# Down projection of a quantised feed-forward: half-tile quantisation moved to GpSimd, and a new order of casts

## The chip, the cores and the metric

The kernel runs on one core of a Trainium2 chip. The metric is the device time of one launch in microseconds (us). The kernel before was timed in three runs: median 204.54 us, from 204.34 to 204.71.

## The reference, cut to what matters

The input x is (32, 128, 256) float32. Two residual layers follow one another: a gated, two-directional RWKV mix of a context with weights `w` and `u`, and a quantised feed-forward. Only the second one, and of it only its last projection, is touched here:

```
x  = x + tanh(g_xattn) * birwkv(layernorm(x), ctx, ctx, w, u)
xq = fake_quant(layernorm(x))                  # one scale for the whole tensor
h  = silu(xq @ Wg.T) * (xq @ Wu.T)             # 4096 tokens x 704
s  = sigmoid(clip_down) * max|h| / 127         # one scale for the whole tensor
hq = clip(round(h / s), -128, 127) * s
x  = x + tanh(g_ffn) * hq @ fake_quant(Wd).T   # 704 -> 256
```

`max|h|` is taken over everything, so nothing of the last product can begin before all of h is there. The weights are quantised as h is, with a scale for each row.

## The kernel before, in words

The program is written engine by engine, with semaphores set and awaited by hand; there is no scheduler, and each engine does its instructions in the order in which they are written. The stages are: statistics and exponentials of the context, the mixing by matrix products (until about 102 us), the second layernorm and its transposes (to about 124 us), gate and up products with silu and the peaks of h (to about 172 us), and then the down stage, which is all that changes.

**The down stage** works on 4 blocks of 1024 tokens (`BLOCKS`), each with 4 outputs of 256 tokens (`OUTS`), 16 outputs in all (`SUMS`). The 704 hidden values stand as 5 full tiles of 128 (`KI`) and a last tile of 64, the *half tile*. Of that one, the two halves of a block's tokens lie above one another, so it is one instruction of 128x512 for the whole block; the 5 full tiles of an output are one instruction of 128x1280, of an output pair 128x2560.

For each piece there are two steps:

- Quantise (L709 on ScalarE, L970 on VectorE): float32 `hidden` times the inverse scale, written as int16, which rounds. The list `QUANTS` has the pieces in the order in which ScalarE does them, as (block, first output, end, first tile, end). `BY_DVE` names the pieces that VectorE quantises itself: the first two, and the half tile of block 1.
- Cast (L986, `cast_h`, VectorE): clip to -128..127 and write bf16. The list `CASTS` is its order. For the half tiles and for outputs 0 and 1 of block 0, source and destination are the same place in `hq` (`z_t` in the trace). All other outputs go through `pair_int`, two buffers of an output pair in `h8_space`, so the cast reads `h_space` in rows of 256 and writes `z_t`.

TensorE then makes an output (`down`, L1183) from 12 products of 128x256. VectorE scales it out of PSUM (`evict`, L992). GpSimd adds it to `x_all` (L502) for the outputs 0 to 14, and SyncE sends each of these out (L358). VectorE itself adds output 15 (L998), whose transfer ScalarE's queue issues (L713).

**Order on VectorE** (L1000 to L1016): before `evict(n)` it casts all that `needed(n + 2)` asks for (for n = 0 and 1, `needed(n + 1)`). `needed` (L195) is a position in `CASTS`: a block's half tile must be cast before its output 0. So the order runs evict 1, quantise and cast half tile 1, cast output 3, cast output 4, evict 2; later evict 5, cast half tile 2, cast output 8, evict 6; and evict 9, cast half tile 3, cast output 12, evict 10. TensorE waits at output n for the same `needed(n)` casts (L1176).

**Order on ScalarE** (L710): `QUANTS`. Before the first piece of an output pair from pair 3 on it waits until the pair two before has been cast. Outputs 4 and 5 are single pieces, outputs 6 and 7 one pair. From block 2 on, the half tile comes first, then two pairs.

**Order on GpSimd** (L499): the adds 0 to 14 and nothing else, each behind `ffn_done`, which the eviction of the same output sets.

Semaphores that the change touches: `h_int` (pieces quantised by ScalarE), `h_int_own` (by VectorE), `hq_done` (casts done), `down_done` (outputs made by TensorE), `inv_done` (the inverse scale is there).

Of the kernel before, what the change touches and what calls it, by code (L numbers as in the profile page):

```python
# [22 lines left out]
ALU = mybir.AluOpType  # L23
# [5 lines left out]
I16 = mybir.dt.int16  # L29
# [6 lines left out]
def wait(engine, semaphore, value):  # L36

    if isinstance(value, int) and value <= 0:
        return
    engine.wait_ge(semaphore, value)  # L40

def gated_rwkv_ffn(nc, x, ctx_kv, g_xattn, g_ffn, w, u, clip_x, clip_down, w_gate, w_up, w_down, out):
# [8 lines left out]
    KI = I // P  # L51
    IR = I - KI * P
    KA = KI + 1
    BT = 1024
    BLOCKS = TOK // BT
# [16 lines left out]
    with ExitStack() as stack:  # L72
# [3 lines left out]
        def sem(name):  # L76
            return stack.enter_context(nc.semaphore(name))
# [95 lines left out]
        def z_bank(g):  # L173
            return (2, 6, 0)[g % 3]

        OUTS = BT // 256
        OUT = KI * 256

        CASTS = [(0, 0, 0, 2), (0, 0, 2, 4), (0, 0, 4, KI), (0, 0, KI, KA), (0, 1, 0, KI), (0, 2, 0, KI), (1, 0, KI, KA), (0, 3, 0, KI)] \
            + [c for b in range(1, BLOCKS) for c in ([(b, 0, KI, KA)] if b > 1 else []) + [(b, i, 0, KI) for i in range(OUTS)]]  # L180

        QUANTS = [(0, 0, 1, 4, KI), (0, 0, OUTS, KI, KA), (0, 1, 2, 0, KI), (0, 2, 3, 0, KI), (0, 3, 4, 0, KI),
                  (1, 0, 1, 0, KI), (1, 1, 2, 0, KI), (1, 2, 4, 0, KI)] \
            + [q for b in range(2, BLOCKS) for q in [(b, 0, OUTS, KI, KA), (b, 0, 2, 0, KI), (b, 2, 4, 0, KI)]]
        BY_DVE = [0, 1, CASTS.index((1, 0, KI, KA))]

        def kept(b, i, k, end):

            if k == KI:
                return hq[b % 2][:, OUTS * OUT:HB]  # L190
            return hq[b % 2][:, i * OUT + k * 256:i * OUT + end * 256]

        def inner(b, i, last, k, end):

            if k == KI:  # L195
                return hidden[:, b * HB + KI * BT:(b + 1) * HB]
            return hidden[:, b * HB:b * HB + KI * BT].rearrange("p (k n) -> p k n", n=BT)[:, k:end, i * 256:last * 256]

        def needed(n):

            return 1 + max(m for m, (b, i, k, _) in enumerate(CASTS) if b == n // OUTS and i == n % OUTS or b < n // OUTS
                           or b == n // OUTS and k == KI)
# [12 lines left out]
        def group(tile, g):  # L215
# [5 lines left out]
        S = {n: small[:, i:i + 1] for i, n in enumerate(names)}  # L221
# [21 lines left out]
        s = {n: sem(n) for n in (  # L243

            "gate_in", "up_in", "down_in", "g_x_in", "g_f_in", "clx_in", "cld_in", "w_in", "u_in",
            "ones_set", "ident_set", "flip_set", "lags_set", "lag_done", "lag_stored", "lag_abs_set", "lag_abs_done", "w_all_in", "u_all_in", "u_all_done", "own_done", "made_exp", "made",
            "tanh_done", "clips_done", "prep",

            "w_rec", "w_quant", "w_cast", "w_turned", "w_stored",

            "ctx_back", "ek_done", "pk_done", "ab_done", "den_done", "ln_done", "rden_done", "ln_half", "rden_half", "mix_done", "x1_done", "x1_own",
# [6 lines left out]
            "scale_x", "inv_x_done", "x_int_own", "x_int_act", "x_int_pool", "xq_done", "gate_done", "up_done", "silu_done", "up_kept", "h_even", "h_odd",  # L258
            "hpeak_done", "h_top_done", "h_topT", "row_ps",

            "inv_done", "h_int", "h_int_own", "hq_done", "pad_set", "diag_done", "row_kept", "down_done", "ffn_done", "sum_done", "dve_sum_done", "out_done")}

        x_in = [sem(f"x_in{g}") for g in range(GROUPS)]
        ring_in = [sem(f"ring_in{i}") for i in range(SLOTS)]
# [97 lines left out]
        def _(pool):  # L362
# [114 lines left out]
            def quantise_x(n):  # L477

                pool.wait_ge(s["x_int_own"], 3)
                pool.wait_ge(s["x_int_act"], 2)  # L480
                nc.gpsimd.tensor_scalar(x_int(n), x_normed(n), S["inv_x"], 1.0, ALU.mult, ALU.mult).then_inc(s["x_int_pool"], 1)
# [10 lines left out]
            for b in range(BLOCKS):  # L492
                for i in range(EVEN):
                    multiply(b, i)
                if b == 0:
                    for n in X_BY_POOL[2:]:
                        quantise_x(n)

            for n in pool_sums:  # L499
                pool.wait_ge(s["ffn_done"], n + 1)  # L500
                xs = x_all[:, n * 2 * C:(n + 1) * 2 * C]
                nc.gpsimd.tensor_tensor(xs, xs, ffn[n // 4 % 2][:, n % 4, :], ALU.add).then_inc(s["sum_done"], 1)  # L502
# [3 lines left out]
        def _(act):  # L506
# [190 lines left out]
            act.wait_ge(s["inv_done"], 1)  # L697
            for b, i, last, k, end in QUANTS:
                pair, first = (b * OUTS + i) // 2, i % 2 * 256
                if k == KI:  # L700
                    wait(act, s["down_done"], OUTS * (b - 1))
                    dst = kept(b, i, k, end).bitcast(I16)
                elif pair == 0:
                    dst = kept(b, i, k, end).bitcast(I16).rearrange("p (k n) -> p k n", n=256)
                else:
                    if pair >= 3 and first == 0:
                        act.wait_ge(s["hq_done"], needed(2 * (pair - 2) + 1))
                    dst = pair_int[pair % 2][:, :, first:first + (last - i) * 256]
                nc.scalar.activation(dst, inner(b, i, last, k, end), ACT.Copy, scale=S["inv_h"]).then_inc(s["h_int"], 1)  # L709
# [7 lines left out]
        def _(dve):  # L717
# [250 lines left out]
            def quantise_h(b, i, k, end):  # L968
                dst = kept(b, i, k, end).bitcast(I16)
                nc.vector.tensor_scalar(dst if k == KI else dst.rearrange("p (k n) -> p k n", n=256), inner(b, i, i + 1, k, end),  # L970
                                        S["inv_h"], None, ALU.mult).then_inc(s["h_int_own"], 1)

            def cast_h(n):

                b, i, k, end = CASTS[n]
                dst = kept(b, i, k, end)
                src = dst.bitcast(I16)
                if n in BY_DVE:
                    dve.wait_ge(s["h_int_own"], BY_DVE.index(n) + 1)
                else:  # L980
                    done = [m for m, (at_, first, last, k0, k1) in enumerate(QUANTS)
                            if at_ == b and (k0, k1) == (k, end) and first <= i < last]
                    dve.wait_ge(s["h_int"], done[0] + 1)
                if k < KI and b * OUTS + i >= 2:
                    src = pair_int[(b * OUTS + i) // 2 % 2][:, :, i % 2 * 256:(i % 2 + 1) * 256]
                nc.vector.tensor_scalar(dst, src, QMAX, -QMAX - 1.0, ALU.min, ALU.max).then_inc(s["hq_done"], 1)  # L986

            def evict(n):
                dve.wait_ge(s["down_done"], n + 1)
                wait(dve, s["sum_done"], len([i for i in pool_sums if i <= n - 8]))  # L990
                dst = ps[:, n % 8, :] if n in dve_sums else ffn[n // 4 % 2][:, n % 4, :]
                nc.vector.scalar_tensor_tensor(dst, ps[:, n % 8, :], S["out_scale"], flat_row, ALU.mult, ALU.mult) \  # L992
                    .then_inc(s["ffn_done"], 1)

            def add_rest(n):
                dve.wait_ge(s["ffn_done"], n + 1)
                xs = x_all[:, n * 2 * C:(n + 1) * 2 * C]
                nc.vector.tensor_tensor(xs, xs, ps[:, n % 8, :], ALU.add).then_inc(s["dve_sum_done"], 1)  # L998

            cast = 0  # L1000
            for n in BY_DVE[0:2]:
                quantise_h(*CASTS[n])
                cast_h(n)
                cast += 1
# [2 lines left out]
            dve.wait_ge(s["row_kept"], 1)  # L1007
            for n in range(SUMS):
                while cast < needed(min(n + (1 if n < 2 else 2), SUMS - 1)):
                    if cast == BY_DVE[2]:  # L1010
                        quantise_h(*CASTS[cast])
                    cast_h(cast)
                    cast += 1
                evict(n)
                if n in dve_sums:
                    add_rest(n)  # L1016
# [195 lines left out]
```

## Time and profile before

| | |
|---|---|
| median of three runs | 204.54 us |
| the profiled execution | 204.7 us |
| its span | 203.0 us (1.7 us lie around it) |
| mean granted TensorE clock | 0.946 |
| TensorE busy, matmul | 172.6 us (85%) |
| VectorE busy | 158.7 us (78%) |
| ScalarE busy | 150.9 us (74%) |
| GpSimd busy | 123.3 us (61%) |

Times in the trace count from the start of the span. The busy times are sums over stages with different limits; the down stage is the stretch from about 172 us to the end. In the trace DVE is VectorE, ACT is ScalarE, POOL is GpSimd, PE is TensorE and SP is SyncE. A row of the timeline may join several instructions of a kind that follow one another closely (x2, x3); its time is then that from the first one's start to the last one's end.

### The profile page before, as it was taken

How to read it: one execution, taken by the hardware profiler on the slowest of the kernel's cores; microseconds unless marked ns; L12 is line 12 of the kernel's file. 1: busy time of each engine (PE TensorE's matmuls, PEld its weight loads, DVE VectorE, ACT ScalarE, POOL GpSimd, SP SyncE). 2: the span in 40 equal slices, each digit the busy share in tenths (PEclk: the TensorE clock that was granted, in tenths of full speed). 3: DMA queues.
4: the chain of work that ended last, by engine and by line, in shares of the span. 5: the costliest groups of instructions: out<-in, count | busy, mean ns of one | idle time of the engine just before them, and what ended most of it. 6: DMA issues, size and time to landing. Idle time of an engine off the chain costs nothing.

```text
span 203.0 us, 3345 instructions
## 1 busy us (share of the span) xinstructions
PE 172.6 (85%) x1146; PEld 126.3 (62%) x1146; DVE 158.7 (78%) x355; ACT 150.9 (74%) x219; POOL 123.3 (61%) x149
## 2 busy tenths in 40 slices
PE   4589995997999999999137998999999996869990
PEld 4447642997989999999136664444343442558770
DVE  0657769174955878998969957599999998999992
ACT  3447969857599379558879998999888980999900
POOL 3365303467869936354788850889876762258892
PEclk9958999999999999999955599999999999999998
DMA  2999999999999999990000000000000000034555
GB/s 73 353 338 353 348 341 292 294 297 289 294 290 323 238 289 293 290 243 0 2 0 0 0 3 2 0 0 0 3 0 0 0 0 0 3 103 164 198 171 195
DMA packets 46448, 30.88 MB, mean 152 GB/s; under 512 B 2272, under 2 KB 46176, under 8 KB 46432
## 3 DMA queue, kind: packets, MB, share of 16 engines
q1 hardware_dynamic: 46016, 30.16, 53.0%
q10 hardware_dynamic: 416, 0.52, 0.7%
q8 instruction: 9, 0.15, 0.3%
q14 instruction: 7, 0.06, 0.1%
HBM read 26.22 MB, written 4.46 MB: 151 GB/s over the span
## 4 chain that ended last, share of the span: by engine, by line
PE 40%; DVE 29%; DMA 10%; ACT 7%; issue 6%; POOL 4%; SPq 1%; POOLq 1%; DVEq 0%
PE ps L1044 21%; DMA hidden<-lag_w 6%; PE ps L1147 6%; DVE h_peaks L937 6%; DVE z_t L986 6%; PE ps L1028 5%; DVE hidden L926 4%; DMA hidden<-in_ctx 4%; PE ps L1075 3%; PE ps L1068 2%; DVE bn L755 2%; DVE z_t L992 2%; DVE hidden L729 2%; DVE silu_out L992 2%; POOL rs L398 2%
## 5 line engine op out<-in xcount | busy, mean ns | idle before, releaser
L1044 PE MATMUL ps<-hidden 128*128 128x128 f32 (+1 forms) x512 | 58.4, 275 | 4.2 <-DVE hidden L729 2.5
L1044 PEld LDWEIGHTS ps<-hidden 128*128 128x128 f32 x512 | 57.7, 192 | 5.4 <-issue 3.3
L428 POOL TENSOR_TENSOR x_all<-x_all,silu_out 128x512 f32<-128x512 f32 x15 | 23.0, 1533 | 17.2 <-DVE silu_out L798 17.2
L937 DVE TENSOR_REDUCE h_peaks<-hidden 128x1 f32<-128x1024 f32 (+1 forms) x24 | 26.1, 1124 | 0.2
L1183 PE MATMUL ps<-wdT,z_t 128*128 128x256 bf16 x192 | 22.4, 272 | 2.8 <-DVE z_t L986 2.5
L786 DVE SCALAR_TENSOR_TENSOR h_space<-z_t,ps 128x256 f32<-128x256 f32 x32 | 18.9, 595 | 7.1 <-PE ps L1044 6.8
L1183 PEld LDWEIGHTS ps<-wdT,z_t 128*128 128x128 bf16 x192 | 17.8, 97 | 7.6 <-DVE z_t L986 3.2
L689 ACT ACTIVATE silu_out<-ps,mix_scale 128x1024 f32<-128x1024 f32 (+1 forms) x18 | 18.3, 1019 | 2.1 <-PE ps L1147 2.0
L1068 PE MATMUL ps<-ident,hidden 128*128 128x128 f32 x64 | 12.1, 352 | 8.9 <-POOL hidden L467 8.2
L1028 PE MATMUL ps<-hidden,flip 128*128 128x512 f32 x32 | 16.7, 662 | 3.3 <-DMA hidden<-in_ctx 3.3
L798 DVE SCALAR_TENSOR_TENSOR silu_out<-ps,small,silu_out 128x256 f32<-128x256 f32 x32 | 15.2, 478 | 5.2 <-ACT silu_out L545 4.6
L534 ACT ACTIVATE z_t<-x_all,mr,nr 128x256 f32<-128x256 f32 x32 | 16.4, 588 | 3.7 <-POOL mr L390 3.7
L747 DVE BATCH_NORM_STATS2 bn<-x_all 128x6 f32<-128x256 f32 x32 | 11.2, 413 | 8.7 <-DMA x_all<-in_x 8.4
L1068 PEld LDWEIGHTS ps<-ident,hidden 128*128 128x128 f32 x64 | 10.2, 185 | 11.5 <-ACT hidden L564 10.0
L709 ACT ACTIVATE h_space<-hidden,small 128x2560 int16<-128x2560 f32 (+1 forms) x9 | 17.1, 1943 | 0.3 <-DVE z_t L986 0.3
L542 ACT ACTIVATE up_out<-h_space 128x512 f32<-128x512 f32 x15 | 9.4, 626 | 10.5 <-DVE h_space L786 10.5
L487 POOL TENSOR_TENSOR hidden<-h_space 128x1024 f32<-128x1024 f32 x6 | 14.7, 2449 | 3.9 <-ACT h_space L693 3.9
L502 POOL TENSOR_TENSOR x_all<-x_all,z_t 128x512 f32<-128x512 f32 x8 | 10.4, 1296 | 10.3 <-DVE z_t L992 9.9
L487 POOL TENSOR_TENSOR hidden<-silu_out,up_out 128x1024 f32<-128x1024 f32 x6 | 14.2, 2363 | 3.8 <-ACT up_out L693 3.8
L926 DVE SCALAR_TENSOR_TENSOR hidden<-ps,mix_scale,silu_out 128x1024 f32<-128x1024 f32 (+1 forms) x12 | 13.2, 1101 | 2.9 <-ACT silu_out L689 2.8
L385 POOL TENSOR_TENSOR ve<-mv,consts 128x4 f32<-128x4 f32 x8 | 1.6, 199 | 21.9 <-DVE mv L751 21.9
L1075 PEld LDWEIGHTS ps<-ident,flip 128*128 128x128 f32 x64 | 10.9, 256 | 5.3 <-POOL ident_b L374 2.8
(117 smaller groups left out, 346.1 us busy)
## 6 DMA issues: line engine op xcount, KB each, us to landing
hidden<-lag_w SPq DMA_DIRECT2D x29, 512.0 KB, 7.4
x_all<-in_x SPq DMA_DIRECT2D x8, 512.0 KB, 8.8
hidden<-in_ctx SPq DMA_DIRECT2D x8, 512.0 KB, 9.3
out<-x_all SPq DMA_DIRECT2D x15, 256.0 KB, 2.1
xq<-in_L_ffn_w_down SPq DMA_DIRECT2D x1, 704.0 KB, 6.1
xq<-in_L_ffn_w_gate SPq DMA_DIRECT2D x1, 640.0 KB, 6.8
h_space<-in_L_ffn_w_up SPq DMA_DIRECT2D x1, 640.0 KB, 5.9
out<-x_all ACTq DMA_DIRECT2D x1, 256.0 KB, 2.7
```

What stands on the lines that cost most here:

```text
L428: nc.gpsimd.tensor_tensor(xs, xs, mixed[:, m % 2, :, :].rearrange("p c b -> p b c"), ALU.add).then_inc(s["x1_done"], 1)
L487: nc.gpsimd.tensor_tensor(hidden[:, b * HB + k * BT:b * HB + (k + 1) * BT], silu_even[n % 2], up_even[n % 2], ALU.mult).then_inc(s["h_even ...
L689: nc.scalar.activation(silu_out[:, 1, 0:cols] if k % 2 else silu_even[even % 2], banks[0], ACT.Silu, scale=mix_scale[:, 0, k:k + 1]).then_ ...
L709: nc.scalar.activation(dst, inner(b, i, last, k, end), ACT.Copy, scale=S["inv_h"]).then_inc(s["h_int"], 1)
L786: nc.vector.scalar_tensor_tensor(den[:, m % 2, i * HALF:(i + 1) * HALF].rearrange("p (c b) -> p c b", b=SEQS), ez[:, :, j * CK:(j + 1) * C ...
L926: nc.vector.scalar_tensor_tensor(hidden[:, b * HB + k * BT:b * HB + k * BT + cols], ps[:, 6:8, :].rearrange("p a n -> p (a n)")[:, 0:cols] ...
L937: nc.vector.tensor_reduce(h_peaks[:, KA * b + k:KA * b + k + 1], hidden[:, b * HB + k * BT:b * HB + k * BT + cols], AX.X, ALU.max, apply_a ...
L1028: last = nc.tensor.matmul(turned(g)[:, half], flip[:, :], ring[g % SLOTS][:, half], start=True, stop=True)
L1044: last = nc.tensor.matmul(ps[:, j % BANKS, c * 2 * SEQS:end * 2 * SEQS], lag_tile(j)[:, c, :], ekp[:, (j * CK + c) * 2 * SEQS:(j * CK + en ...
L1068: last = nc.tensor.transpose(ps[:, z_bank(g) + h, i * T:(i + 1) * T], z_all[:, n * C + h * P:n * C + (h + 1) * P], ident[:, :])
L1075: nc.tensor.matmul(ps[:, TURN, 0:P], flip[:, :], ident[:, :], start=True, stop=True)
L1183: last = nc.tensor.matmul(ps[:, n % 8, j * C:(j + 1) * C], hq[b % 2][:, at_:at_ + P], wdT[:, tile, :], start=(k == 0 and j == 0), stop=(k ...
```

## The change

The half tiles of blocks 1, 2 and 3 are quantised by GpSimd, by a `tensor_scalar` of 128x512 in a new function `quantise_half`. It does the one of block 1 before its first add, as soon as the inverse scale is there and three casts are done; that of block 2 between the adds 3 and 4; that of block 3 between the adds 8 and 9. VectorE's casts of these tiles wait on the new semaphore `h_int_pool`. VectorE no longer quantises half tile 1, and ScalarE no longer those of blocks 2 and 3. In `CASTS`, output 3 now stands ahead of half tile 1. In `QUANTS`, the outputs 6 and 7 are two single pieces instead of a pair.

```diff
--- before.py
+++ after.py
@@ -176,13 +176,14 @@
         OUTS = BT // 256
         OUT = KI * 256
 
-        CASTS = [(0, 0, 0, 2), (0, 0, 2, 4), (0, 0, 4, KI), (0, 0, KI, KA), (0, 1, 0, KI), (0, 2, 0, KI), (1, 0, KI, KA), (0, 3, 0, KI)] \
-            + [c for b in range(1, BLOCKS) for c in ([(b, 0, KI, KA)] if b > 1 else []) + [(b, i, 0, KI) for i in range(OUTS)]]
-
-        QUANTS = [(0, 0, 1, 4, KI), (0, 0, OUTS, KI, KA), (0, 1, 2, 0, KI), (0, 2, 3, 0, KI), (0, 3, 4, 0, KI),
-                  (1, 0, 1, 0, KI), (1, 1, 2, 0, KI), (1, 2, 4, 0, KI)] \
-            + [q for b in range(2, BLOCKS) for q in [(b, 0, OUTS, KI, KA), (b, 0, 2, 0, KI), (b, 2, 4, 0, KI)]]
-        BY_DVE = [0, 1, CASTS.index((1, 0, KI, KA))]
+        CASTS = [(0, 0, 0, 2), (0, 0, 2, 4), (0, 0, 4, KI), (0, 0, KI, KA)] + [(0, i, 0, KI) for i in range(1, OUTS)] \
+            + [c for b in range(1, BLOCKS) for c in [(b, 0, KI, KA)] + [(b, i, 0, KI) for i in range(OUTS)]]
+
+
+        QUANTS = [(0, 0, 1, 4, KI), (0, 0, OUTS, KI, KA)] + [(0, i, i + 1, 0, KI) for i in range(1, OUTS)] \
+            + [(1, i, i + 1, 0, KI) for i in range(OUTS)] \
+            + [(b, i, i + 2, 0, KI) for b in range(2, BLOCKS) for i in range(0, OUTS, 2)]
+        BY_DVE = [0, 1]
 
         def kept(b, i, k, end):
 
@@ -258,7 +259,7 @@
             "scale_x", "inv_x_done", "x_int_own", "x_int_act", "x_int_pool", "xq_done", "gate_done", "up_done", "silu_done", "up_kept", "h_even", "h_odd",
             "hpeak_done", "h_top_done", "h_topT", "row_ps",
 
-            "inv_done", "h_int", "h_int_own", "hq_done", "pad_set", "diag_done", "row_kept", "down_done", "ffn_done", "sum_done", "dve_sum_done", "out_done")}
+            "inv_done", "h_int", "h_int_own", "h_int_pool", "hq_done", "pad_set", "diag_done", "row_kept", "down_done", "ffn_done", "sum_done", "dve_sum_done", "out_done")}
 
         x_in = [sem(f"x_in{g}") for g in range(GROUPS)]
         ring_in = [sem(f"ring_in{i}") for i in range(SLOTS)]
@@ -496,7 +497,18 @@
                     for n in X_BY_POOL[2:]:
                         quantise_x(n)
 
+            def quantise_half(b):
+
+                wait(pool, s["down_done"], OUTS * (b - 1))
+                nc.gpsimd.tensor_scalar(kept(b, 0, KI, KA).bitcast(I16), inner(b, 0, OUTS, KI, KA), S["inv_h"], 1.0,
+                                        ALU.mult, ALU.mult).then_inc(s["h_int_pool"], 1)
+
+            pool.wait_ge(s["inv_done"], 1)
+            pool.wait_ge(s["hq_done"], 3)
+            quantise_half(1)
             for n in pool_sums:
+                if n in (OUTS, 2 * OUTS + 1):
+                    quantise_half(2 + n // (2 * OUTS))
                 pool.wait_ge(s["ffn_done"], n + 1)
                 xs = x_all[:, n * 2 * C:(n + 1) * 2 * C]
                 nc.gpsimd.tensor_tensor(xs, xs, ffn[n // 4 % 2][:, n % 4, :], ALU.add).then_inc(s["sum_done"], 1)
@@ -698,7 +710,6 @@
             for b, i, last, k, end in QUANTS:
                 pair, first = (b * OUTS + i) // 2, i % 2 * 256
                 if k == KI:
-                    wait(act, s["down_done"], OUTS * (b - 1))
                     dst = kept(b, i, k, end).bitcast(I16)
                 elif pair == 0:
                     dst = kept(b, i, k, end).bitcast(I16).rearrange("p (k n) -> p k n", n=256)
@@ -977,6 +988,8 @@
                 src = dst.bitcast(I16)
                 if n in BY_DVE:
                     dve.wait_ge(s["h_int_own"], BY_DVE.index(n) + 1)
+                elif k == KI and b > 0:
+                    dve.wait_ge(s["h_int_pool"], b)
                 else:
                     done = [m for m, (at_, first, last, k0, k1) in enumerate(QUANTS)
                             if at_ == b and (k0, k1) == (k, end) and first <= i < last]
@@ -998,7 +1011,7 @@
                 nc.vector.tensor_tensor(xs, xs, ps[:, n % 8, :], ALU.add).then_inc(s["dve_sum_done"], 1)
 
             cast = 0
-            for n in BY_DVE[0:2]:
+            for n in BY_DVE:
                 quantise_h(*CASTS[n])
                 cast_h(n)
                 cast += 1
@@ -1007,8 +1020,6 @@
             dve.wait_ge(s["row_kept"], 1)
             for n in range(SUMS):
                 while cast < needed(min(n + (1 if n < 2 else 2), SUMS - 1)):
-                    if cast == BY_DVE[2]:
-                        quantise_h(*CASTS[cast])
                     cast_h(cast)
                     cast += 1
                 evict(n)
```

## Rows read from the trace of the kernel before

**Rows 1.** Busy time in one stretch: PE, PEld, DVE, ACT, POOL, clock, DMA share, GB/s.
```profile
179.84:197.80 17.96, 17.80 (x156) 14.60 (x156) 17.62 (x28) 13.02 (x7) 14.94 (x12) 1.00 0.48 163
```

**Rows 2.** Waits from 172 us to the end: us in total, times, longest.
```profile
PE ps L1183 <- DVE z_t L986: 2.5, 3, 1.7
...
DVE ps L992 <- PE ps L1183: 0.3, 1, 0.3
```

**Rows 3.** Timeline of DVE, first outputs: start, duration, instruction, idle before.
```profile
173.86 0.43 DVE L986 TENSOR_SCALAR z_t<-z_t 128x256 bf16<-128x256 int16 x2
174.56 0.49 DVE L986 TENSOR_SCALAR z_t<-z_t 128x1280 bf16<-128x1280 int16 x1 [0.28 <-ACT z_t L709]
...
176.64 0.75 DVE L992 SCALAR_TENSOR_TENSOR z_t<-ps,small,down_row 128x512 f32<-128x512 f32 x1
177.30 0.48 DVE L970 TENSOR_SCALAR z_t<-hidden,small 128x512 int16<-128x512 f32 x1
177.82 1.24 DVE L986 TENSOR_SCALAR z_t<-z_t 128x512 bf16<-128x512 int16 x1
178.98 1.53 DVE L986 TENSOR_SCALAR z_t<-h_space 128x1280 bf16<-128x1280 int16 x2
180.43 0.73 DVE L992 SCALAR_TENSOR_TENSOR z_t<-ps,small,down_row 128x512 f32<-128x512 f32 x1
```

**Rows 4.** Timeline of DVE around half tile 2.
```profile
183.20 0.73 DVE L992 SCALAR_TENSOR_TENSOR silu_out<-ps,small,down_row 128x512 f32<-128x512 f32 x1
...
184.59 0.73 DVE L992 SCALAR_TENSOR_TENSOR silu_out<-ps,small,down_row 128x512 f32<-128x512 f32 x1
185.25 0.27 DVE L986 TENSOR_SCALAR z_t<-z_t 128x512 bf16<-128x512 int16 x1
185.44 0.80 DVE L986 TENSOR_SCALAR z_t<-h_space 128x1280 bf16<-128x1280 int16 x1
186.17 0.73 DVE L992 SCALAR_TENSOR_TENSOR silu_out<-ps,small,down_row 128x512 f32<-128x512 f32 x1
```

**Rows 5.** Timeline of POOL in the down stage.
```profile
175.80 1.28 POOL L502 TENSOR_TENSOR x_all<-x_all,z_t 128x512 f32<-128x512 f32 x1 [6.86 <-DVE z_t L992]
177.47 1.44 POOL L502 TENSOR_TENSOR x_all<-x_all,z_t 128x512 f32<-128x512 f32 x1 [0.39 <-DVE z_t L992]
...
195.49 3.87 POOL L502 TENSOR_TENSOR x_all<-x_all,silu_out 128x512 f32<-128x512 f32 x3
```

**Rows 6.** POOL's multiplications L487 (ns min/median/max), and the timeline at its longest.
```profile
L487 POOL TENSOR_TENSOR hidden<-h_space x6: 2357/2368/2869, 132.9 to 166.6; 128x1024 f32<-128x1024 f32 x6
...
132.90 0.68 DVE L907 TENSOR_SCALAR z_t<-z_t 128x2048 bf16<-128x2048 int16 x1
...
132.94 2.87 POOL L487 TENSOR_TENSOR hidden<-h_space 128x1024 f32<-128x1024 f32 x1 [0.28 <-ACT h_space L693]
```

**Rows 7.** POOL's three forms of tensor_scalar: ns min/median/max, first and last start.
```profile
L450 POOL TENSOR_SCALAR xq<-xq x1: 405/405/405, 41.0 to 41.0; 128x256 f32<-128x256 f32 x1
...
L467 POOL TENSOR_SCALAR hidden<-x_all,rs,mr x8: 548/554/557, 104.0 to 119.5; 128x256 f32<-128x256 f32 x8
...
L481 POOL TENSOR_SCALAR z_t<-z_t,small x4: 1107/1120/1615, 127.6 to 139.8; 128x1024 int16<-128x1024 f32 x4
```

**Rows 8.** Timeline of PE, last half of output 1.
```profile
175.78 0.82 PE L1183 MATMUL ps<-wdT,z_t 128*128 128x256 bf16 x6
```

**Rows 9.** Timeline: POOL's own pace, and VectorE released by POOL.
```profile
138.74 2.21 POOL L481 TENSOR_SCALAR z_t<-z_t,small 128x1024 int16<-128x1024 f32 x2
...
108.98 0.55 POOL L467 TENSOR_SCALAR hidden<-x_all,rs,mr 128x256 f32<-128x256 f32 x1
...
109.64 1.22 DVE L813 TENSOR_REDUCE peaks<-hidden 128x1 f32<-128x1024 f32 x1 [0.23 <-POOL hidden L467]
```

**Rows 10.** Timeline of ACT in the down stage.
```profile
174.44 5.11 ACT L709 ACTIVATE h_space<-hidden,small 128x1280 int16<-128x1280 f32 x4
...
182.15 0.71 ACT L709 ACTIVATE z_t<-hidden,small 128x512 int16<-128x512 f32 x1
```

## Prediction

> **What bounds the kernel now.** I read the busy shares first, then the down stage: its busy times, its waits, and the timelines of VectorE, GpSimd and ScalarE there. From 179.84 us to the last product VectorE is busy 17.62 of 17.96 us, TensorE 17.80, GpSimd 14.94, ScalarE 13.02 [rows 1]. Two engines look full, and the waits decide between them: VectorE waits for TensorE only 0.3 us, once, at the last output, while TensorE waits for VectorE's casts 2.5 us, 1.7 of them in one piece [rows 2]. So VectorE's order of casts and evictions sets the pace: an eviction every 1.39 us (183.20 to 184.59), and 1.58 us where a half tile is cast between (184.59 to 186.17) [rows 4]. Whatever moves one eviction moves all that follow, down to the last transfer, since VectorE has no idle time in which to make it up. GpSimd's adds take 1.28 us and start 0.83 us after the start of their eviction (176.64 to 177.47) [rows 3, 5], so they end 0.11 us before the next is due: close, but behind VectorE. The last three, back to back, end at 195.49 + 3.87 = 199.36 us [rows 5].
>
> The row to look at is the cast of half tile 1: 1.24 us at 177.82, where the same form takes 0.27 at 185.25 [rows 3, 4]. GpSimd's add ran from 177.47 to 178.91, and the cast ended 0.15 us behind it. The other way round, a multiplication of GpSimd that began 0.04 us after a contiguous cast of VectorE took 2.87 us against a median of 2.37 [rows 6]. So a contiguous cast of VectorE and an instruction of GpSimd exclude one another. The casts of output 3 and later read `h_space` in rows of 256, and take 0.80 us with an add beside them: they don't meet it.
>
> **The change, part by part.** I count by the starts of evictions.
>
> *A GpSimd half tile.* No row has this form (128x512, float32 to int16). The nearest: 128x256 at 0.405 and 0.55, and the same operation at 128x1024 at 1.107 [rows 7]. I take 0.65, near the straight line between 0.405 and 1.107 (0.64); these two are the ends. Below nothing it can't go, since VectorE waits for it.
>
> *Start, half tile 1.* GpSimd waits for the third cast, in the pair that ends at 174.29 [rows 3]; so about 174.1, plus 0.09 to wake: its tile runs from 174.2 to about 174.85. The cast of output 1, contiguous too, is issued at 174.56 and would be held until then; it ends 0.15 us later as half tile 1 does, plus 0.20, by which its form is longer (0.49 against 0.29): 175.20 against 175.05. Eviction 0 slips by as much and is covered by the wait for ScalarE's output 2. Eviction 1 is not: TensorE ends output 1 at 176.60 [rows 8], now 176.75. Cost 0.15 us; bounds 0 and 0.61 by the ends above.
>
> *The turn to block 1.* Now: eviction 1 at 176.64, quantise 0.48, held cast until 179.06, casts of outputs 3 and 4, eviction 2 at 180.43 [rows 3]. After: eviction 1 at 176.79, then output 3's cast, which runs beside add 1 at no cost; add 1 from 177.62 to 178.90 (1.28, as VectorE's quantise no longer stretches it to 1.44); the half tile's cast is issued in it, is held, ends at 179.05; then only one cast, starting 0.08 before that end, 0.73 long: eviction 2 at 179.70. Gain 0.73 us. TensorE's wait of 1.7 us for output 3 shrinks, which alone is worth nothing, since VectorE is late behind it.
>
> *Half tile 2.* With eviction 5 as zero: add 3 from -1.95 to -0.67, GpSimd's tile to -0.02, add 4 to 1.26. VectorE issues its cast at 0.66, in the middle of add 4, while before the cast fell between two adds, and took 0.27 us [rows 4]. Now held, it ends at 1.41, and eviction 6 comes 0.65 later, at 2.06 instead of 1.58. Cost 0.48 us.
>
> *Half tile 3.* It stands one add later. With eviction 9 as zero: add 8 from -0.56 to 0.72, the tile to 1.37, but VectorE wants to cast it at 0.66. It must wait for the semaphore, and behind it on VectorE stand the cast of output 12 and eviction 10, on which TensorE and add 10 wait. At 1.37 add 9 has long been released (eviction 9 ended at 0.74). GpSimd starts a ready instruction with no gap (2.21 us for two of 1.107), VectorE woke 0.11 us after GpSimd's end (108.98 + 0.55 = 109.53, start 109.64) [rows 9]. So add 9 is there first and holds the cast until 1.37 + 1.28 = 2.65; it ends at 2.80, eviction 10 at 3.45 instead of 1.58. Cost 1.87 us.
>
> The trace has no case in which both want to start at once; here a rule bears on it. The Trainium skill, "SBUF — State Buffer", section "Who interferes with whom", says that issue order alone decides which of the two gets the shared pair of ports, for its whole instruction. The trace agrees in the two collisions [rows 3, 5, 6]. By the rule the cost is the 1.87 us above; if VectorE's waiting cast went first whatever the order, it would be 0.82, the rival below.
>
> *ScalarE.* It loses two half tiles (0.71 us each) and does outputs 6 and 7 singly, at some 1.25 each [rows 10]: output 6 is ready at about 180.8, needed at 181.7; output 7 at 182.1, needed at 183.1. It costs nothing, and gains nothing, since VectorE waited for it only at 174.56. Were this cover gone, its lateness would show in full on VectorE's casts; there is near 1 us of it.
>
> *Added waits on GpSimd.* `down_done` is met in both places, as the add before implies it. Transfers move with their adds. At the end GpSimd has caught up, since VectorE was held longer than it: nothing.
>
> **Sum.** -0.73 + 0.48 + 1.87 = +1.62 us on the profiled execution: span 203.0 to 204.6, time 204.7 to 206.3. The profile lies 0.16 above the median of 204.54, so 206.2. With 0.405 us for the tile: -0.88 + 0.23 + 1.63 = +0.98, 205.5. With 1.107: -0.27 + 0.94 + 2.33 = +3.0, 207.5. The second needs a half tile as dear as a double one.
>
> **Rivals.**
>
> *A. VectorE's cast of half tile 3 gets in before add 9.* Then it starts at 1.48, and eviction 10 follows 0.92 after the cast's start as in [rows 4]: 2.40, cost 0.82, sum +0.57: 205.1. For it: the margin is 0.1 us of semaphore and start-up times that no row shows for this pair. Against: [rows 9].
>
> *B. GpSimd's queue keeps the port.* At half tile 2, add 5 is ready when add 4 ends; in the collisions of the trace nothing was ready behind. If add 5 also passes the held cast, another 1.28 us: sum +2.9, 207.4. Against: VectorE has been asking for 0.6 us by then.
>
> *C. Faster: nothing is held.* If the 1.24 us of the cast were something else, bound to that place, then: no 0.15, output 3's cast at 177.30, the half tile's at 178.03, output 4 ready from ScalarE at 178.3 [rows 10], eviction 2 at 179.05, a gain of 1.38; nothing at half tile 2; 0.82 at half tile 3. Sum -0.56: 204.0. It decides if a contiguous cast under an add takes 0.3 us. Against: two independent pairs of rows that agree to 0.1 us.
>
> *D. No difference.* A tile near 0.4 us together with A: -0.88 + 0.23 + 0.58 = -0.07, 204.5.
>
> **How the numbers follow.** Forecast (add 9 first, VectorE next at half tile 2) 0.62; A 0.18; B 0.07; C 0.07; D and other mixtures 0.06. Range 204.9 to 207.2: it takes in the forecast, A, and a tile up to about 1.0 us, and leaves out B, C and D. Of changes of this kernel 0.2% (0.4 us) can be told from none. Slower: forecast, B and most of A, 0.84. Within: D and the rest of A, 0.09. Faster: C, 0.07.
>
> **What would show it.** In the trace after: GpSimd's `tensor_scalar` of 128x512 at about 0.65 us, three times; eviction 2 about 0.7 us earlier; the cast of half tile 2 recorded at about 0.75 us; idle time on VectorE before the cast of half tile 3, and that cast itself over 1 us, with eviction 10 some 3.4 us after eviction 9; a gap of about 1.9 us on TensorE before output 12. I am wrong if the cast of half tile 3 takes 0.3 us (A), if that of half tile 2 takes 2 us (B), or if half tile 1's takes 0.3 us beside an add (C). And if evictions from 10 on come closer than 1.39 us, VectorE was not the bound.

## The result, and the profile after

The changed kernel takes 206.09 us (median of five runs, 205.77 to 206.96) against 204.54 us before (204.09 to 205.36). The ratio, taken over all runs, is 1.0092, with a 95% interval of 1.0061 to 1.0122: slower by 1.9 us, 1.2 to 2.5. (The two medians differ by 1.55 us.) The forecast was 206.2, the range 204.9 to 207.2. The profiled execution took 206.96 us, its span is 204.8 us; it is the slowest of the five, and 0.23 us of its distance to the kernel before lie ahead of the down stage.

Part of the loss stands in no timeline. The time of a launch is longer than its span, and this rest grew: it is 2.07 to 2.19 us in the five runs of the changed kernel (mean 2.12), and 1.68 to 1.86 us in the runs of the kernel before that were timed beside the experiments (mean 1.74). So the change costs 0.38 us outside the span besides what it costs in the down stage. The ratios and these means leave out three slow executions (355.81 us of e4, 301.24 and 207.03 us of the kernel before).

Single executions of these kernels differ by some tenths of a per cent. The steps are therefore read inside the down stage. Zero is the start of VectorE's first quantise of h; a number behind a half tile is its block, and output n, its eviction n and its add n belong together. These are the zero and the turn to block 3 in the timeline of VectorE, for the kernel before:

```profile
172.22 0.49 DVE L970 TENSOR_SCALAR z_t<-hidden,small 128x512 int16<-128x512 f32 x1
...
190.33 0.73 DVE L992 SCALAR_TENSOR_TENSOR z_t<-ps,small,down_row 128x512 f32<-128x512 f32 x1
190.99 0.27 DVE L986 TENSOR_SCALAR z_t<-z_t 128x512 bf16<-128x512 int16 x1
...
191.91 0.73 DVE L992 SCALAR_TENSOR_TENSOR z_t<-ps,small,down_row 128x512 f32<-128x512 f32 x1
```

The same timeline of the changed kernel. L981 is the quantise, L999 the cast, L1005 the eviction; these rows answer to [rows 3, 4]:

```profile
172.45 0.49 DVE L981 TENSOR_SCALAR z_t<-hidden,small 128x512 int16<-128x512 f32 x1
...
174.80 0.73 DVE L999 TENSOR_SCALAR z_t<-z_t 128x1280 bf16<-128x1280 int16 x1 [0.28 <-ACT z_t L720]
...
177.11 0.75 DVE L1005 SCALAR_TENSOR_TENSOR z_t<-ps,small,down_row 128x512 f32<-128x512 f32 x1 [0.20 <-PE ps L1194]
177.78 0.81 DVE L999 TENSOR_SCALAR z_t<-h_space 128x1280 bf16<-128x1280 int16 x1
178.51 0.86 DVE L999 TENSOR_SCALAR z_t<-z_t 128x512 bf16<-128x512 int16 x1
179.29 0.81 DVE L999 TENSOR_SCALAR z_t<-h_space 128x1280 bf16<-128x1280 int16 x1
180.02 0.74 DVE L1005 SCALAR_TENSOR_TENSOR z_t<-ps,small,down_row 128x512 f32<-128x512 f32 x1
...
184.17 0.74 DVE L1005 SCALAR_TENSOR_TENSOR silu_out<-ps,small,down_row 128x512 f32<-128x512 f32 x1
184.83 0.72 DVE L999 TENSOR_SCALAR z_t<-z_t 128x512 bf16<-128x512 int16 x1
...
186.20 0.73 DVE L1005 SCALAR_TENSOR_TENSOR silu_out<-ps,small,down_row 128x512 f32<-128x512 f32 x1
...
190.35 0.73 DVE L1005 SCALAR_TENSOR_TENSOR z_t<-ps,small,down_row 128x512 f32<-128x512 f32 x1
191.76 1.35 DVE L999 TENSOR_SCALAR z_t<-z_t 128x512 bf16<-128x512 int16 x1 [0.67 <-POOL z_t L503]
193.03 0.81 DVE L999 TENSOR_SCALAR z_t<-h_space 128x1280 bf16<-128x1280 int16 x1
193.76 0.73 DVE L1005 SCALAR_TENSOR_TENSOR z_t<-ps,small,down_row 128x512 f32<-128x512 f32 x1
```

Eviction 2 comes at 7.57 us from zero instead of 8.21 (0.64 gained). Evictions 5 and 6 are 2.03 us apart instead of 1.58 (0.45 lost), evictions 9 and 10 3.41 instead of 1.58 (1.83 lost). Eviction 10 is at 21.31 instead of 19.69: 1.62 us later, and this stays to the end of VectorE's last instruction (28.68 us from zero instead of 27.06).

GpSimd's timeline shows what each long cast ran into. L503 is the new quantise, L514 the add; these rows answer to [rows 5]:

```profile
174.50 0.69 POOL L503 TENSOR_SCALAR z_t<-hidden,small 128x512 int16<-128x512 f32 x1 [5.32 <-DVE z_t L999]
...
177.94 1.27 POOL L514 TENSOR_TENSOR x_all<-x_all,z_t 128x512 f32<-128x512 f32 x1 [0.39 <-DVE z_t L1005]
...
183.47 0.69 POOL L503 TENSOR_SCALAR z_t<-hidden,small 128x512 int16<-128x512 f32 x1
...
184.13 1.27 POOL L514 TENSOR_TENSOR x_all<-x_all,silu_out 128x512 f32<-128x512 f32 x1
...
185.36 1.31 POOL L514 TENSOR_TENSOR x_all<-x_all,silu_out 128x512 f32<-128x512 f32 x1
...
191.03 0.69 POOL L503 TENSOR_SCALAR z_t<-hidden,small 128x512 int16<-128x512 f32 x1
191.69 1.27 POOL L514 TENSOR_TENSOR x_all<-x_all,z_t 128x512 f32<-128x512 f32 x1
```

Every cast of a `z_t` piece that begins beside one of these instructions ends 0.15 to 0.34 us behind it: the cast of output 1 behind the tile (175.53 and 175.19), those of half tiles 1, 2 and 3 behind adds 1 (179.37 and 179.21), 4 (185.55 and 185.40) and 9 (193.11 and 192.96). The 14 casts out of `h_space` take 0.802 to 0.807 us, with adds beside them (least, median and most in ns):

```profile
L999 DVE TENSOR_SCALAR z_t<-h_space x14: 802/804/807, 176.1 to 197.2; 128x1280 bf16<-128x1280 int16 x14
L999 DVE TENSOR_SCALAR z_t<-z_t x8: 227/509/1354, 173.0 to 191.8; 128x512 bf16<-128x512 int16 x6, 128x256 bf16<-128x256 int16 x1, 128x1280 bf16<-128x1280 int16 x1
```

TensorE waits for output 12's cast, its one long gap of the stage (idle time in brackets):

```profile
193.99 0.71 PE L1194 MATMUL ps<-wdT,z_t 128*128 128x256 bf16 x5 [1.94 <-DVE z_t L999]
```

### The profile page after: what moved, and what is told of

It reads as the page before. It is cut to its first block, busy times and chain, and to the rows that moved or that the text cites. A ratio compares the mean times of both kernels' runs of the same rounds, so it can differ in the third digit from the quotient of the medians.

```text
span 204.8 us, 3347 instructions
## 1 busy us (share of the span) xinstructions
PE 171.3 (84%) x1146; PEld 124.7 (61%) x1146; DVE 159.7 (78%) x354; ACT 149.8 (73%) x218; POOL 125.1 (61%) x152
## 4 chain that ended last, share of the span: by engine, by line
PE 37%; DVE 26%; DMA 10%; ACT 8%; SPq 6%; issue 5%; POOL 5%; POOLq 1%; DVEq 0%
PE ps L1055 18%; PE ps L1039 8%; PE ps L1158 6%; DMA hidden<-lag_w 6%; DVE h_peaks L948 6%; DVE z_t L999 5%; DVE hidden L937 4%; DMA hidden<-in_ctx 4%; ACT hidden L576 3%; PE ps L1086 3%; SPq L306 2%; DVE bn L766 2%; POOL x_all L514 2%; ACT z_t L583 2%; DVE z_t L1005 2%
## 5 line engine op out<-in xcount | busy, mean ns | idle before, releaser
L1194 PE MATMUL ps<-wdT,z_t 128*128 128x256 bf16 x192 | 22.9, 273 | 3.9 <-DVE z_t L999 3.8
L720 ACT ACTIVATE h_space<-hidden,small 128x1280 int16<-128x1280 f32 (+1 forms) x10 | 17.1, 1777 | 1.1 <-DVE z_t L999 1.1
L766 DVE BATCH_NORM_STATS2 bn<-x_all 128x6 f32<-128x128 f32 x64 | 13.6, 279 | 0.1
L1086 PEld LDWEIGHTS ps<-ident,flip 128*128 128x128 f32 x64 | 10.3, 242 | 5.3 <-POOL ident_b L375 2.8
```

The source lines that it names most:

```text
L766: return nc.vector.bn_stats(bn2[:, n, h, :], x_all[:, n * C + h * P:n * C + (h + 1) * P])
L1194: last = nc.tensor.matmul(ps[:, n % 8, j * C:(j + 1) * C], hq[b % 2][:, at_:at_ + P], wdT[:, tile, :], start=(k == 0 and j == 0), stop=(k ...
```

## The experiments

All times "from zero" are as above, each from one trace. The ratios are to the kernel before, timed again beside the experiments (medians 204.44 us beside e1, e2, e3 and e6, and 204.30 us beside e4, e5 and e7), with their 95% intervals. "The port" in the expectations is the way to the on-chip memory that VectorE and GpSimd are taken to share.

**Half tile 3 one add earlier (e1).** The changed kernel, with this edit:

```diff
-                if n in (OUTS, 2 * OUTS + 1):
+                if n in (OUTS, 2 * OUTS):
                     quantise_half(2 + n // (2 * OUTS))
```

> The changed kernel with half tile 3 quantised by GpSimd before add 8 instead of before add 9. Theory (an add of GpSimd and a contiguous cast of VectorE exclude one another, whoever starts first): with eviction 9 as zero the tile ends at 0.0, add 8 runs from 0.0 to 1.28, the cast is issued at 0.66, is held, ends at 1.42; eviction 10 at 2.05 instead of 3.41 us, as at half tile 2. The whole comes 1.36 us below the changed kernel, about 204.7 us. Rival (what costs is only that the tile comes too late, 0.67 us of waiting and what follows from it; the port plays no part): the tile is there 0.66 us early, so nothing is left of the cost, eviction 10 at 1.58, the whole 1.83 us below, 204.3 us. Second rival (GpSimd's load as such sets the pace): no difference to the changed kernel.

Measured: 204.99 us, ratio 1.0039 (1.0011 to 1.0067). The timeline of VectorE and GpSimd at the turn to block 3:

```profile
189.84 1.27 POOL L514 TENSOR_TENSOR x_all<-x_all,z_t 128x512 f32<-128x512 f32 x1
189.89 0.73 DVE L1005 SCALAR_TENSOR_TENSOR z_t<-ps,small,down_row 128x512 f32<-128x512 f32 x1
...
190.55 0.71 DVE L999 TENSOR_SCALAR z_t<-z_t 128x512 bf16<-128x512 int16 x1
191.07 1.32 POOL L514 TENSOR_TENSOR x_all<-x_all,z_t 128x512 f32<-128x512 f32 x1
...
191.91 0.74 DVE L1005 SCALAR_TENSOR_TENSOR z_t<-ps,small,down_row 128x512 f32<-128x512 f32 x1
```

The evictions 9 and 10 are 2.02 us apart: 2.05 by the port, 1.58 if only lateness cost, 3.41 if GpSimd's load did. The run's time agrees once the rest outside the span is counted: eviction 10 is 0.22 us behind the kernel before, the rest is 2.09 us instead of 1.74, together 0.57 us; measured are 0.2 to 1.4 us by the ratio. The tile had long been there (its quantise began at 189.18 and took 0.70), and VectorE shows no wait; the cast is long because add 8 runs. The rows also settle a point that the prediction left to a rival. Add 9 was ready when add 8 ended at 191.11, since eviction 9 had ended at 190.62. The cast ended at 191.26 all the same, 0.15 us behind add 8 and not one add later, and add 9 is recorded with 1.32 instead of 1.27 us. The waiting cast had its turn first.

**Add 9 made to wait for the cast (e2).** The changed kernel, with one wait more:

```diff
                     quantise_half(2 + n // (2 * OUTS))
+                if n == 2 * OUTS + 1:
+                    pool.wait_ge(s["hq_done"], CASTS.index((3, 0, KI, KA)) + 1)
                 pool.wait_ge(s["ffn_done"], n + 1)
```

> The changed kernel, with one more wait: GpSimd starts add 9 only when VectorE has cast half tile 3. Theory (add 9 holds the port for 1.28 us when the cast wants it): the cast starts 0.04 us behind the tile, at 1.41 from eviction 9, takes 0.27 to 0.29 us instead of 1.35, and eviction 10 comes at 2.33 instead of 3.41 us; about 1.1 us below the changed kernel, 205.0 us. Rival (the cast takes 1.35 us because GpSimd has written its source just before, or for another reason of its own): the cast stays at 1.3 us, eviction 10 at 3.4 or later, no gain. In both, add 9 starts late, at about 1.8, and nothing waits for it.

Measured: 205.54 us, ratio 1.0045 (1.0023 to 1.0068). The timeline at the same turn:

```profile
190.47 0.73 DVE L1007 SCALAR_TENSOR_TENSOR z_t<-ps,small,down_row 128x512 f32<-128x512 f32 x1
...
191.15 0.70 POOL L503 TENSOR_SCALAR z_t<-hidden,small 128x512 int16<-128x512 f32 x1
191.88 0.29 DVE L1001 TENSOR_SCALAR z_t<-z_t 128x512 bf16<-128x512 int16 x1 [0.68 <-POOL z_t L503]
...
192.26 1.28 POOL L516 TENSOR_TENSOR x_all<-x_all,z_t 128x512 f32<-128x512 f32 x1 [0.41 <-DVE z_t L1001]
...
192.82 0.74 DVE L1007 SCALAR_TENSOR_TENSOR z_t<-ps,small,down_row 128x512 f32<-128x512 f32 x1
```

The cast of the same tile, written by the same engine just before, takes 0.29 us instead of 1.35 once nothing of GpSimd runs beside it, and eviction 10 comes 2.35 us after eviction 9 (2.33 expected). So 1.83 us of cost divide into 1.06 for the held cast and 0.77 for the tile that comes late. A wait put in made the stage faster than that of the changed kernel. The median lies 0.5 us above the 205.0 that was expected, which was reckoned from the changed kernel's median of five runs. Eviction 10, at 20.25, is 1.06 below the changed kernel as expected. Reckoned from the kernel before, the time fits: 0.56 us in the down stage and 0.27 outside the span (2.01 us against 1.74) make a ratio of 1.0041, measured 1.0045. So the 0.5 us lie in the spread of the changed kernel's few runs, as far as the record shows.

**Half tiles 2 and 3 back on ScalarE (e3).** Only the first part of the change is left. ScalarE does every output from block 1 on singly.

```diff
-            + [(b, i, i + 2, 0, KI) for b in range(2, BLOCKS) for i in range(0, OUTS, 2)]
+            + [q for b in range(2, BLOCKS) for q in [(b, 0, OUTS, KI, KA)] + [(b, i, i + 1, 0, KI) for i in range(OUTS)]]
...
-                if n in (OUTS, 2 * OUTS + 1):
-                    quantise_half(2 + n // (2 * OUTS))
...
                 if k == KI:
+                    wait(act, s["down_done"], OUTS * (b - 1))
...
-                elif k == KI and b > 0:
+                elif k == KI and b == 1:
```

> The changed kernel with half tiles 2 and 3 back on ScalarE, and all outputs from block 1 on quantised singly there; only half tile 1 stays on GpSimd, and output 3 is still cast ahead of it. Theory: the first part of the change gains 0.64 us by itself and the other two tiles cost 0.45 and 1.83 us, so evictions 5 to 6 and 9 to 10 are 1.58 us apart again, and the whole is 2.3 us below the changed kernel and 0.64 below the kernel before: about 203.9 us. Rival (ScalarE had no room, so the tiles had to leave it): ScalarE needs 4 x 1.25 + 0.61 = 5.6 us for a block and VectorE 5.75, so it can't fall behind by this count; if it does, VectorE shows waits for ScalarE before the casts of block 2, and the gain shrinks by their sum.

Measured: 203.88 us, ratio 0.9979 (0.9958 to 1.0000). The timeline of VectorE at the turn to block 2:

```profile
184.11 0.74 DVE L1004 SCALAR_TENSOR_TENSOR silu_out<-ps,small,down_row 128x512 f32<-128x512 f32 x1
184.77 0.28 DVE L998 TENSOR_SCALAR z_t<-z_t 128x512 bf16<-128x512 int16 x1
...
185.70 0.74 DVE L1004 SCALAR_TENSOR_TENSOR silu_out<-ps,small,down_row 128x512 f32<-128x512 f32 x1
```

Evictions 5 to 6 and 9 to 10 are 1.59 us apart, eviction 2 is at 7.56, eviction 10 at 19.04, 0.65 ahead of the kernel before. VectorE never waits for ScalarE in blocks 1 to 3. The whole loss of the change sits in the two later tiles, and so does the longer rest outside the span: it is back at 1.76 us. The run's time by itself hardly tells e3 from no change, as the interval ends at 1.0000; the trace does.

**The order of casts alone (e6).** The kernel before, VectorE still quantising half tile 1:

```diff
-        CASTS = [..., (0, 2, 0, KI), (1, 0, KI, KA), (0, 3, 0, KI)] \
+        CASTS = [..., (0, 2, 0, KI), (0, 3, 0, KI), (1, 0, KI, KA)] \
```

> The kernel before with only the order of casts changed: output 3 ahead of half tile 1, which VectorE still quantises itself. Theory: output 3's cast (0.73 us) runs under add 1; then VectorE's own quantise, which is contiguous too, is issued in the last 0.7 us of the add and held until it ends, 178.75 on the clock of the kernel before; it ends at 179.04, its cast at 179.33, and eviction 2 comes at about 179.98 instead of 180.43: 0.45 us gained of the 0.64 that the changed kernel gained there, about 204.1 us. Rival (the gain is that of the quantise that VectorE no longer does, 0.52 us, and the order is worth nothing because TensorE has room): eviction 2 at 180.4, no difference.

Measured: 204.07 us, ratio 0.9984 (0.9958 to 1.0009): the run's time can't tell it from no change, the trace can. Its timeline of VectorE, first output 3's cast, then the quantise (L970) and the cast of half tile 1, and GpSimd's add 1:

```profile
177.22 0.81 DVE L986 TENSOR_SCALAR z_t<-h_space 128x1280 bf16<-128x1280 int16 x1
177.38 1.27 POOL L502 TENSOR_TENSOR x_all<-x_all,z_t 128x512 f32<-128x512 f32 x1 [0.40 <-DVE z_t L992]
177.95 0.99 DVE L970 TENSOR_SCALAR z_t<-hidden,small 128x512 int16<-128x512 f32 x1
178.97 0.29 DVE L986 TENSOR_SCALAR z_t<-z_t 128x512 bf16<-128x512 int16 x1
```

Eviction 2 is at 7.78 from zero (8.21 before): 0.43 of the 0.64 us come from the order, because output 3's cast fills time in which a contiguous piece would be held anyway. The quantise itself is now held: it takes 0.99 us against 0.48 and ends at 178.94, 0.29 us behind add 1. So VectorE's contiguous quantise is held as the cast is, in the one case traced.

**GpSimd's half tile 1 behind the cast of output 1 (e4).** As e3, with this edit:

```diff
-            pool.wait_ge(s["hq_done"], 3)
+            pool.wait_ge(s["hq_done"], 5)
             quantise_half(1)
```

> As e3, but GpSimd starts half tile 1 only behind the fifth cast (output 1), not the third. Zero is the first quantise of VectorE. Theory: output 1's cast is no longer held (0.49 us instead of 0.73), half tile 1 runs in GpSimd's idle time from 2.9 to 3.6, just ahead of add 0, and eviction 1 comes at 4.42 as in the kernel before instead of 4.66; eviction 2, still behind the held cast, at 7.33 instead of 7.56: 0.23 us below e3. Rival (eviction 1 is late for another reason, as TensorE's pace): eviction 1 stays at 4.66.

Measured: 203.40 us, ratio 0.9949 (0.9931 to 0.9968). The timeline of VectorE and GpSimd at the cast of output 1 and the tile:

```profile
174.85 0.49 DVE L998 TENSOR_SCALAR z_t<-z_t 128x1280 bf16<-128x1280 int16 x1 [0.28 <-ACT z_t L719]
...
175.52 0.69 POOL L503 TENSOR_SCALAR z_t<-hidden,small 128x512 int16<-128x512 f32 x1 [6.31 <-DVE z_t L998]
```

The cast of output 1 takes 0.49 us again, eviction 1 is at 4.42 and eviction 2 at 7.33. So the tile's early start did cost 0.24 us at eviction 1 (4.66 in the changed kernel).

**And half tile 1 cast ahead of output 3 (e5).** As e4, with the order of casts of the kernel before:

```diff
-        CASTS = [...] + [(0, i, 0, KI) for i in range(1, OUTS)] \
-            + [c for b in range(1, BLOCKS) for c in [(b, 0, KI, KA)] + [(b, i, 0, KI) for i in range(OUTS)]]
+        CASTS = [...] + [(0, 1, 0, KI), (0, 2, 0, KI), (1, 0, KI, KA), (0, 3, 0, KI)] \
+            + [c for b in range(1, BLOCKS) for c in ([(b, 0, KI, KA)] if b > 1 else []) + [(b, i, 0, KI) for i in range(OUTS)]]
```

> As e4, but with the order of casts of the kernel before: half tile 1 ahead of output 3. Theory: the cast of the half tile is issued right behind eviction 1, in the gap before add 1, and takes 0.28 us instead of being held; eviction 2 comes at 4.42 + 0.66 + 0.19 + 0.73 + 0.73 = 6.73, or at 6.83 with the wait for output 4 from ScalarE (ready at 6.07), against 8.21 in the kernel before and 7.33 in e4: 1.4 us below the kernel before, about 203.1 us. Rival (output 3 must come first, as the change has it, or TensorE runs late): eviction 2 or 3 waits for TensorE, and the gain over e4 is lost. Second rival (the GpSimd tile grips the port all the same): the cast stays above 0.8 us.

Measured: 202.82 us, ratio 0.9935 (0.9914 to 0.9956), the lowest median of all. Its timeline, of VectorE and of GpSimd's add 1:

```profile
173.19 0.49 DVE L980 TENSOR_SCALAR z_t<-hidden,small 128x512 int16<-128x512 f32 x1
...
177.64 0.75 DVE L1004 SCALAR_TENSOR_TENSOR z_t<-ps,small,down_row 128x512 f32<-128x512 f32 x1
178.31 0.28 DVE L998 TENSOR_SCALAR z_t<-z_t 128x512 bf16<-128x512 int16 x1
178.47 1.27 POOL L512 TENSOR_TENSOR x_all<-x_all,z_t 128x512 f32<-128x512 f32 x1 [0.34 <-DVE z_t L1004]
...
180.03 0.74 DVE L1004 SCALAR_TENSOR_TENSOR z_t<-ps,small,down_row 128x512 f32<-128x512 f32 x1
```

The cast starts behind eviction 1 and 0.16 us ahead of add 1, and takes 0.28 us. It ends 0.12 us behind the add's start, and the add takes its usual 1.27 us. Eviction 2 is at 6.84 (6.83 expected), 1.37 us ahead of the kernel before, and no eviction waits for TensorE but the last. The order "output 3 first" of the change is the worse one as soon as GpSimd, and not VectorE, quantises the tile early. By eviction 2 this beats e4 by 0.49 us and by the medians by 0.6; the intervals of the two ratios overlap, so their order rests on the traces.

**Single pieces on ScalarE alone (e7).** The kernel before with this edit:

```diff
-                  (1, 0, 1, 0, KI), (1, 1, 2, 0, KI), (1, 2, 4, 0, KI)] \
-            + [q for b in range(2, BLOCKS) for q in [(b, 0, OUTS, KI, KA), (b, 0, 2, 0, KI), (b, 2, 4, 0, KI)]]
+                  (1, 0, 1, 0, KI), (1, 1, 2, 0, KI), (1, 2, 3, 0, KI), (1, 3, 4, 0, KI)] \
+            + [q for b in range(2, BLOCKS) for q in [(b, 0, OUTS, KI, KA)] + [(b, i, i + 1, 0, KI) for i in range(OUTS)]]
```

> The kernel before with only ScalarE's list changed: from output 6 on all outputs are quantised singly instead of in pairs. Theory: ScalarE is ahead of VectorE either way, so every eviction stays where it is, eviction 2 at 8.21 and eviction 10 at 19.69 from the first quantise, to 0.05 us. Rival (single pieces cost ScalarE 0.17 us per pair, and its lead is thin, so VectorE begins to wait for it in block 2): eviction 10 some tenths later.

Measured: 204.10 us, ratio 0.9994 (0.9970 to 1.0018). Eviction 2 at 8.22, eviction 10 at 19.70: nothing, as expected. So the gains of e3, e4 and e5 don't come from ScalarE's list.

| from zero, us | eviction 1 | eviction 2 | 5 to 6 | 9 to 10 | eviction 10 |
|---|---|---|---|---|---|
| before | 4.42 | 8.21 | 1.58 | 1.58 | 19.69 |
| changed | 4.66 | 7.57 | 2.03 | 3.41 | 21.31 |
| e1: tile 3 at add 8 | 4.65 | 7.56 | 2.03 | 2.02 | 19.91 |
| e2: add 9 behind the cast | 4.66 | 7.56 | 2.04 | 2.35 | 20.25 |
| e3: tiles 2, 3 on ScalarE | 4.66 | 7.56 | 1.59 | 1.59 | 19.04 |
| e6: order alone | 4.42 | 7.78 | 1.59 | 1.58 | 19.25 |
| e4: tile 1 behind cast 1 | 4.42 | 7.33 | 1.58 | 1.59 | 18.80 |
| e5: and ahead of output 3 | 4.45 | 6.84 | 1.59 | 1.58 | 18.32 |
| e7: singles alone | 4.42 | 8.22 | 1.59 | 1.59 | 19.70 |

## Why the prediction was right

**VectorE's order is the bound.** Right. In all nine kernels the shifts of the evictions before it arrive at eviction 10 to within 0.02 us; from eviction 2 on VectorE waits only for a tile of GpSimd that comes late (0.67 and 0.68 us) and 0.34 to 0.37 us for TensorE at output 15.

**GpSimd's tile, 0.65 us.** Measured 0.692 to 0.695 in three of three. The straight line between the two nearest forms was 0.04 us low, and GpSimd made up for it at the later two by starting each ready instruction about 0.03 us before the recorded end of the one before: the tile of half tile 3 ended 1.37 us after eviction 9's start, as reckoned.

**Start, 0.15 us.** Measured 0.24, by the 0.20 us that VectorE now waits for TensorE at eviction 1. From zero, the tile ran from 2.05 to 2.74 us where 1.98 to 2.63 was reckoned: 0.07 later and 0.04 longer. The cast behind it ended 0.34 us after it, as reckoned (0.35). As a share of its size it is the term of the down stage that was off most.

**The turn, gain 0.73.** Measured 0.64; the difference is the 0.09 of the start. From eviction 1 on it was 2.91 us, predicted 2.91 (176.79 to 179.70). The experiments e6 and e3 divide it: 0.43 by the order, 0.22 by the tile's leaving VectorE, net of its early collision.

**Half tile 2, 0.48.** Measured 0.45. Rival B, that GpSimd's next add passes the held cast, is refuted by the cast itself: it took 0.72 us here and 0.71 in e1 and ended 0.15 us behind the add that held it, though the next add was ready. That add is recorded with 1.31 and 1.32 us instead of 1.27, so it gave way.

**Half tile 3, 1.87.** Measured 1.83. The race went as forecast: add 9 started at 191.69, VectorE's cast at 191.76. But the margin is 0.07 us, less than argued: VectorE woke 0.04 us after GpSimd's end, not 0.11. This race was traced once, so no run shows how often it would go the other way. e2 shows what rival A would have been: 2.35 (forecast 2.40). The rule of the Trainium skill ("SBUF — State Buffer", "Who interferes with whom") says that issue order alone decides and that the first has the ports for its whole instruction; this race and every collision above agree with it.

**Rival C, nothing is held**, falls with the same tile's cast at 0.29 and at 1.35 us, with nothing else changed than what GpSimd does beside it.

**The sum, +1.62**, is what eviction 10 shows: 1.62. That it is exact is in part luck: the errors of the terms (+0.09, -0.03, -0.04) nearly cancel.

**The time, 206.2.** Here the hit is luck in a second way. The prediction carried the rest outside the span over unchanged, and it grew by 0.38 us. With it the whole is +2.0 us, as the ratio's 1.9 says, and the forecast would have been about 206.5. The median of 206.09 lies 0.4 us below that, within the spread of the five runs (1.2 us), and so by chance near 206.2.

What stays open: why the rest outside the span grew. It did so in the three kernels in which GpSimd quantises half tiles 2 and 3 between its adds (2.12, 2.09 and 2.01 us) and not in e3, e4 and e5, where it quantises half tile 1 alone (1.76 to 1.80); no row shows the cause. Open too is whether it is the contiguous layout that makes a piece of VectorE meet GpSimd: the pieces held were all contiguous and the casts out of `h_space` never were held, but these differ in their source as well, and no run changed the layout alone. And last, whether an add that reads less, or another operation of GpSimd, holds the port for less than its whole recorded time; this was not tried.

## What to carry to other kernels

In these traces a contiguous cast or quantise of VectorE and an instruction of GpSimd (add, multiplication or quantise) took turns. So before moving work onto GpSimd, write both engines' timelines next to one another and see which of its long instructions will be running when VectorE's next contiguous piece is issued. A GpSimd that looks idle enough by its share (61% here) may have no room at the one moment that counts; a producer there must be done before its consumer is due (here 0.66 us after an eviction's start, and the tile came at 1.37), and must not be followed by a ready long instruction. Place VectorE's contiguous piece right behind the instruction that releases GpSimd's next one: there it cost 0.28 us instead of 0.7 to 1.35. And compare the time of a launch with its span before and after: a cost outside the span is in no timeline.

An instruction that was held showed no idle time and no wait here. Its own duration grew (0.29 to 1.35 us), and the page of the profile books it as busy VectorE time (159.7 us against 158.7 before, with a quantise less).

## What the runs showed of the hardware that was not expected

VectorE's wake-up by GpSimd took 0.04 us here and 0.11 at [rows 9], while GpSimd began its next ready instruction about 0.03 us before the recorded end of the one before (191.03 + 0.69 = 191.72, next at 191.69). So in this race the instruction that waited for GpSimd's semaphore came second, by 0.07 us.

The rest of a launch outside its span grew from 1.74 to 2.12 us, without a row that shows why.
